# Transposes of the identity in TensorE's prologue waits, q/k products of step 0 moved ahead of it, and another order of the first expert scalings

## The chip, the cores and the metric

One core of one Trainium2 chip. The metric is the device time of one execution in microseconds. "TensorE" is PE in the profile, VectorE is DVE, ScalarE is ACT, GpSimd is POOL, SyncE is SP.

## The reference

Input x is (32, 256, 128): 32 batches of 256 tokens with 128 channels. All is in float32.

```python
x = L0_attn_x
xn = _layernorm(x, axis=-1)
x = x + _L0_attn_ref(xn, ...) + _L0_ffn_ref(xn, ...)
# _L0_attn_ref: 16 heads of 8, rotated q and k, decay bias, causal softmax, output projection
# _L0_ffn_ref:
n1 = _layernorm(x, ln1_w, ln1_b)
rw = _gating(n1, smha_sim, smha_gates, 2)              # weights of 8 experts per token
q = einsum('btc,ech,bte->bth', n1, q_proj, rw)         # k and v likewise
attn = softmax(causal(q @ k.T * scale)) @ v
hs = x + einsum('bth,ehc,bte->btc', attn, o_proj, rw)
n2 = _layernorm(hs, ln2_w, ln2_b)
rw2 = _gating(n2, moe_sim, moe_gates, 2)
inter = gelu(einsum('btc,eci->btei', n2, w1))
return hs + einsum('btei,eic,bte->btc', inter, w2, rw2)
```

## The kernel before

Each engine has its own instruction order, written out by hand, and the engines meet at semaphores. An engine works through its order strictly, so an instruction that waits holds all that stands behind it on that engine.

**Prologue.** It loads constants and weights, normalises batches 0 to 2, computes their rotated q and k (`proj` on TensorE, `rotate` on VectorE, in seven links), the gating of batches 0 and 1, and the first pass of scores of batch 0 in six units (`unit1(0, 0, k)`). A row maximum on VectorE follows each unit (`row_max`), and the next unit waits for it. `n1s`, the channels scaled by the gating weights, is made on GpSimd for eight experts; `qk(n, e)` adds expert e's product of q and of k into one PSUM bank (lines 1621 and 1622). `max_T(0)` transposes the maxima (line 1566), `weights_T(b)` the gating weights (line 1523), which ACT then copies out (`evac_weights`, semaphore `rwT_done`) behind the DMAs that it issues itself.

**Attention loop.** 32 steps, one for a batch. Step n on TensorE interleaves the first pass of batch n+1 (`next_max(k)`), the second pass of batch n (`unit2`), the q/k products of batch n (already made for e = 0 to 3 in the prologue where n is 0, by `first_qk`), `pv`, `soft_scores`, the V products `ve`, and the output products `oe`. For each unit of the second pass ACT takes an exponential (line 789) and then writes the seed for the next unit (line 795). The first unit of the first pass also waits until `rotate(n + 2)` has read its bank, and in step 0 nothing of the step starts before `rwT_done` is 2.

**Expert stage.** 16 tiles of 512 tokens in 8 pairs (a, b), 8 experts each. TensorE runs `down(k)` (line 1898) and `up(k + 3)` (line 1884) in turn. ACT takes the gelu of up's result (line 989), VectorE scales it by the gating weights (`scale_gelu`, line 1422), and `down` reads the scaled tile. VectorE also does, between the scalings, the statistics of the norm of a later pair (`layer_norm2`, 17 interruptible pieces, which end at line 1320), the gating of the next pair (31 links, with a call of `beside_gating(k)` behind most of them), and `finish` of the tile before. On ACT the order is fixed by `at`, the number of the gelu in its pair: behind gelus 3 and 4 stand two scalings each of `z2` for tile t (line 841), which wait for the end of the norm; behind gelus 5 and 6 two each for tile t + 1; between gelu 6 and these last two stands the tanh of the gating (line 875), which waits for the subtraction of line 1174.

In pair 0 VectorE's order is: scalings a0, a1, six pieces of the norm, a2, the rest of the norm, the gating with a3 to a7 at links 7, 12, 17, 22 and 27, then b0 and four pieces of the next norm, b1, `finish(a)`, four pieces, b2, and so on.

Of the kernel before, what the change touches and what calls it, by code (L numbers as in the profile page):

```python
# [19 lines left out]
P = 128  # L20
# [38 lines left out]
GATE_LINKS = 21 + 10  # L59
MAX_LINKS = 3  # L60
ATS_CHUNKS = ((0, 1), (1, 1), (2, 2), (4, 2), (6, 2))
GELU_AT = (2, 7, 12, 17, 22, 27)
GATE_MAX_AT = (1, 6, 13, 17)

# [55 lines left out]
def run(steps):  # L120

    for _ in steps:
        pass


def build(nc, x, w_attn, w_o, log_xi, pi_logit, e_logit, ln1_w, ln1_b, ln2_w, ln2_b, sim1, gates1,
# [9 lines left out]
    with ExitStack() as ctx:  # L136
# [7 lines left out]
        ident = sb("ident", [P, P])  # L144
# [100 lines left out]
        ps = ctx.enter_context(nc.psum_tensor("ps", [P, 8, 512], F32))  # L245
# [32 lines left out]
        rwT_done = sem("rwT_done")  # L278
# [738 lines left out]
        def _(dve):  # L1017
# [396 lines left out]
            def scale_gelu(t, e):  # L1414
                k = E * t + e
                dve.wait_ge(gelu_done, k + 1)
                dve.wait_ge((rep2_lo_in, rep2_hi_in)[e // (E // 2)][t % 2], 16 * (t // 2 + 1))
                if k >= 2:
                    dve.wait_ge(moe_out, k - 1)
                else:  # L1420
                    dve.wait_ge(oe_out, NB)
                dve.tensor_tensor(hgs[:, k % 2], hg[:, k % 4], rep2[t % 2][e // (E // 2)][:, e % (E // 2)], ALU.mult  # L1422
                                  ).then_inc(hgs_done, 1)
# [10 lines left out]
            def pair(g):  # L1434
                a, b = 2 * g, 2 * g + 1
                scale_gelu(a, 0)
                scale_gelu(a, 1)
                if g:
                    finish(a - 1)
                else:  # L1440
                    norm = layer_norm2(2)
                    for _ in range(6):
                        next(norm, None)
                    scale_gelu(a, 2)
                    run(norm)

                def beside_gating(k):
                    if k in GELU_AT[(g == 0):]:
                        scale_gelu(a, 2 + GELU_AT.index(k))

                if g + 1 < NP:
                    gating(g + 1, BP, 1, gate2, LG2(g + 1), LG2(g + 1)[:, :, E], 2, beside_gating)
                else:
                    for k in GELU_AT:
                        beside_gating(k)
                norm = layer_norm2(g + 3) if g + 3 < NP else iter(())
                for e in range(E):
                    scale_gelu(b, e)
                    if e == 1:
                        finish(a)  # L1460
                    for _ in range(4):
                        next(norm, None)
                run(norm)
# [6 lines left out]
        @block.tensor  # L1470
        def _(pe):
            mm = pe.matmul

            def plant_seeds():
                pe.wait_ge(cast_done, CASTS)
# [93 lines left out]
            def unit2(n, u, k):  # L1569

                Q, i = divmod(k, 3)
                if k == 0:
                    pe.wait_ge(max_in, 16 * NF * (n + 1))
                if not isinstance(n, int) or UNITS * n + k >= 1:
                    pe.wait_ge(seed_done, UNITS * n + k)
                for h in range(2 if i < 2 else HG):
                    hh = HG * Q + (2 * i if i < 2 else 0) + h
                    for f in range(NF):
                        bank = ps[:, S2[f]]
                        if i < 2:  # L1580
                            ins = mm(bank[:, h * S:(h + 1) * S], kst[ROWS[f], u, hh, 0:P], qst[ROWS[f], u, hh, :],  # L1581
                                     start=False, stop=True, skip_group_check=True)
                        else:
                            ins = mm(bank[:, h * P:(h + 1) * P], kst[ROWS[f], u, hh, P:S], qst[ROWS[f], u, hh, P:S],
                                     start=False, stop=True, skip_group_check=True)
                ins.then_inc(s2_out, 1)
# [27 lines left out]
            def qk(n, e):  # L1614

                pe.wait_ge(n1s_done, E * n + e + 1)
                if e == 0:

                    pe.wait_ge(ve_done, n)
                    pe.wait_ge(v_done, min(n + 2, NB) if isinstance(n, int) else n + 2)  # L1620
                mm(ps[:, QKB, 0:S], wq[:, e], n1s[:, e], start=(e == 0), stop=(e == E - 1), skip_group_check=True)  # L1621
                ins = mm(ps[:, QKB, S:2 * S], wk[:, e], n1s[:, e], start=False, stop=(e == E - 1),  # L1622
                         skip_group_check=True)
                if e == E - 1:
                    ins.then_inc(qk_out, 1)
# [105 lines left out]
            def step(n, u, n_x):  # L1731
                f, g = n + 2, n + 3

                def next_max(k):
                    if n_x:
                        unit1(n + 1, 1 - u, k, f if n_x >= 2 else None)

                def first_qk(e):
                    if not isinstance(n, int) or n > 0:
                        qk(n, e)  # L1740

                next_max(0)
                unit2(n, u, 0)
                first_qk(0)
                first_qk(1)
                if n_x == 0:
                    norm_T2(0)
                first_qk(2)
                if n_x >= 2:
                    logits_T(f, u)  # L1750
                if n_x == 0:
                    norm_T2(1)
                next_max(1)
                unit2(n, u, 1)
                if n_x >= 2:
                    logits(f)
                first_qk(3)
                qk(n, 4)
                next_max(2)
                unit2(n, u, 2)  # L1760
                qk(n, 5)
                if n_x == 0:
                    logits2_T(0)
                qk(n, 6)
                next_max(3)
                unit2(n, u, 3)
                qk(n, 7)
                pv(n, u, 0)
                if n_x == 0:
                    logits2(0)  # L1770
                next_max(4)
                unit2(n, u, 4)
                soft_scores(n)
                ve(n, 0)
                out_T(n, 0)
                ve(n, 1)
                ve(n, 2)
                ve(n, 3)
                next_max(5)
                unit2(n, u, 5)  # L1780
                if n_x == 0:
                    norm_T2(2)
                for e in range(4, E):
                    ve(n, e)
                if n_x == 0:
                    norm_T2(3)
                soft_T(n)
                if n_x == 3:

                    norm_T(g, LATER, lambda: pe.wait_ge(s1_read, UNITS * f))  # L1790
                pv(n, u, 1)
                soft_av(n, (lambda: pe.wait_ge(lg_read, f + 1)) if n_x >= 2 else (lambda: None))
                out_T(n, 1)
                if n_x == 0:
                    weights_T2(0)
                if n_x >= 2:
                    proj_v(f, True)
                if n_x >= 2:

                    weights_T(f, lambda: None)  # L1800
                if n_x:
                    max_T(n + 1)
                att_T(n)
                if n_x == 3:
                    proj(g, LATER, lambda: None)
                if n_x >= 2:

                    pe.wait_ge(rwT_done, f + 1)
                if n_x:
                    pe.wait_ge(mT_done, n + 2)  # L1810
                oe(n, 0)
                oe(n, 1)
                att_out(n)
                oe(n, 2)
                oe(n, 3)
                if n_x == 0:
                    logits2_T(1)
                for e in range(4, E):
                    oe(n, e)
                if n_x == 0:  # L1820
                    logits2(1)
# [10 lines left out]
            logits(0)  # L1832
            proj_v(0, False)
            plant_seeds()
            norm_T(1, FIRST, lambda: pe.wait_ge(lg_read, 1))
            proj(1, FIRST, lambda: pe.wait_ge(rot_chain, 2))
            weights_T(0, lambda: None)
            pe.wait_ge(rows_in, 16 * N_ROWS)
# [4 lines left out]
            logits(1)  # L1843
            proj_v(1, False)
            unit1(0, 0, 2)
            unit1(0, 0, 3)
            unit1(0, 0, 4)
            pe.wait_ge(ld_w, 16 * N_W)
            qk(0, 0)
            qk(0, 1)  # L1850
            unit1(0, 0, 5)
            qk(0, 2)
            qk(0, 3)
            max_T(0)
            norm_T(2, LATER, lambda: pe.wait_ge(s1_read, UNITS))
            proj(2, LATER, lambda: None)
            weights_T(1, lambda: pe.wait_ge(rwT_done, 1))
            pe.wait_ge(rwT_done, 2)
            step(0, 0, 3)
            step(1, 1, 3)  # L1860
            with pe.Fori(1, NB // 2 - 2) as j:
# [106 lines left out]
```

## Time and profile before

| what | us |
|---|---|
| median of 3 runs | 1212.77 (1212.22 to 1213.09) |
| the profiled execution's own time | 1212.19 |
| its span, first to last instruction | 1210.40 |
| mean granted clock of TensorE | 0.994 of full |
| TensorE busy / VectorE / ACT / POOL | 1161.8 / 1018.8 / 717.7 / 245.9 |
| prologue | 0 to 60.13 |
| step 0 | 60.13 to 89.33 |
| step 1 | 89.33 to 117.50 |
| expert stage | from 963.61 |

The span is what the profile shows; the execution's own time is longer by the start and end around it. Stages are told by TensorE's instructions: step n + 1 begins with the first mask product of its first pass. In a row, the number behind a name is how many instructions it merges, and the time in brackets is how long the engine was idle before and who ended it.

### The profile page before, as it was taken

Reading aid. Unit: us, or ns where it says so; the run is one execution under the profiler, and the core shown is the slowest. Engines: PE = TensorE matmul, PEld = TensorE weight load, DVE = VectorE, ACT = ScalarE, POOL = GpSimd, SP = SyncE. Lnnn points to the kernel's source line nnn. Section 1 sums busy time; section 2 is a strip of 40 time slices with the busy share of each in tenths; the row PEclk is TensorE's granted clock in tenths of the full one; section 3 lists DMA queues with packets and bytes.
Section 4 is the critical chain, followed back from the end, with each engine's and each line's share of the span. In section 5 each row is a group of like instructions: output and inputs, shape, how many; then the busy total and the mean of one; then the engine's idle time right before and its main releaser. Section 6 shows DMA issues by size and latency. Waiting matters only on the chain.

```text
span 1210.4 us, 33207 instructions
## 1 busy us (share of the span) xinstructions
PE 1161.8 (96%) x10652; PEld 896.3 (74%) x10652; DVE 1018.8 (84%) x3687; ACT 717.7 (59%) x1292; POOL 245.9 (20%) x374
## 2 busy tenths in 40 slices
PE   2599999999999999999999999999999999999998
PEld 1377777778777788777777777777877667777776
DVE  8889999999999999999999998999876577777664
ACT  5166666666666656666666666666557745555532
POOL 5222222222222232222222222223322000000000
PEclk9989999999999999999999999999999999999999
DMA  4443233333323333233333323333331234444453
GB/s 109 129 125 91 90 94 106 104 108 89 94 93 91 90 94 91 94 92 89 94 106 107 103 90 93 92 91 91 95 93 54 96 151 165 174 176 168 172 189 120
DMA packets 103113, 133.01 MB, mean 110 GB/s; under 512 B 13576, under 2 KB 82424, under 8 KB 94864
## 3 DMA queue, kind: packets, MB, share of 16 engines
q1 hardware_dynamic: 100548, 130.72, 34.6%
q10 hardware_dynamic: 2508, 1.58, 0.5%
q8 instruction: 31, 0.51, 0.2%
q14 instruction: 26, 0.21, 0.1%
HBM read 109.12 MB, written 21.54 MB: 108 GB/s over the span
## 4 chain that ended last, share of the span: by engine, by line
PE 77%; DVE 14%; issue 6%; ACT 1%; ACTq 1%; DVEq 1%; DMA 1%; POOL 0%; SPq 0%; POOLq 0%
PE ps L1621 10%; PE ps L1667 10%; PE ps L1898 9%; PE ps L1622 9%; PE ps L1884 9%; PE ps L1631 5%; PE ps L1494 3%; PE ps L1598 3%; PE ps L1581 2%; PE ps L1557 2%; PE ps L1547 2%; PE ps L1544 2%; DVE att L1249 1%; PE ps L1554 1%; PE ps L1603 1%
## 5 line engine op out<-in xcount | busy, mean ns | idle before, releaser
L1223 DVE TENSOR_REDUCE mx<-ps 128x4 f32<-128x1024 f32 (+1 forms) x192 | 234.8, 1223 | 35.8 <-PE ps L1557 20.7
L789 ACT ACTIVATE pr<-ps 128x1024 f32<-128x1024 f32 x192 | 196.7, 1024 | 77.1 <-PE ps L1581 54.3
L637 POOL TENSOR_TENSOR n1s<-rep,n1T 128x256 f32<-128x256 f32 x256 | 177.3, 731 | 297.8 <-DVE mpart L1237 280.7
L795 ACT ACTIVATE ps<-trn 128x1024 f32<-128x1024 bf16 x191 | 196.5, 1029 | 5.1
L1898 PEld LDWEIGHTS ps<-w2s,ats 128*128 128x128 f32 x1024 | 131.4, 191 | 53.4 <-issue 43.9
L1621 PE MATMUL ps<-n1s,wqk 128*128 128x256 f32 x512 | 164.7, 404 | 1.3 <-issue 1.3
L1622 PE MATMUL ps<-n1s,wqk 128*128 128x256 f32 x512 | 153.8, 382 | 0.0
L989 ACT ACTIVATE n1s<-ps 128x512 f32<-128x512 f32 x128 | 76.6, 598 | 121.3 <-PE ps L1884 120.2
L1898 PE MATMUL ps<-w2s,ats 128*128 128x128 f32 x1024 | 136.1, 276 | 2.9 <-DVE ats L1422 2.8
L1631 PE MATMUL ps<-wv,n1s 128*128 128x128 f32 x1024 | 133.1, 278 | 0.0
L1884 PE MATMUL ps<-rep,w1s 128*128 128x512 f32 x256 | 130.7, 594 | 0.0
L1631 PEld LDWEIGHTS ps<-wv,n1s 128*128 128x128 f32 x1024 | 124.3, 192 | 4.9
L1667 PE MATMUL ps<-wop,ats 128*128 128x128 f32 x1024 | 126.6, 277 | 0.0
L1667 PEld LDWEIGHTS ps<-wop,ats 128*128 128x128 f32 x1024 | 119.6, 192 | 5.7 <-DVE ats L1274 4.6
L1622 PEld LDWEIGHTS ps<-n1s,wqk 128*128 128x128 f32 x512 | 98.4, 192 | 13.8
L1621 PEld LDWEIGHTS ps<-n1s,wqk 128*128 128x128 f32 x512 | 89.3, 195 | 26.0 <-issue 15.9
L742 ACT ACTIVATE n1T<-xzT,lnp 128x256 f32<-128x256 f32 x32 | 19.2, 600 | 108.2 <-POOL n1s L637 108.2
L1274 DVE TENSOR_TENSOR ats<-rep,ps 128x512 f32<-128x512 f32 (+1 forms) x160 | 81.1, 573 | 0.0
L1598 PE MATMUL ps<-pr,vst 128*32 128x256 f32 x1024 | 68.5, 385 | 0.6 <-ACT pr L789 0.6
L644 POOL TENSOR_TENSOR zt<-xn,rstd 128x256 f32<-128x256 f32 x32 | 20.6, 643 | 215.8 <-DVE rstd L1048 215.8
L656 POOL TENSOR_TENSOR bs<-hs,xa 128x256 f32<-128x256 f32 x32 | 23.3, 728 | 200.2 <-DVE hs L1290 200.2
L1422 DVE TENSOR_TENSOR ats<-n1s,stk 128x512 f32<-128x512 f32 x64 | 44.0, 688 | 14.0 <-PE ps L1898 13.9
(229 smaller groups left out, 2051.4 us busy)
## 6 DMA issues: line engine op xcount, KB each, us to landing
rep<-scr_rw SPq DMA_DIRECT2D x32, 1024.0 KB, 5.6
stk<-scr_rw SPq DMA_DIRECT2D x16, 1024.0 KB, 8.2
scr_parts<-parts SPq DMA_DIRECT2D x64, 192.0 KB, 5.8
stk<-scr_parts SPq DMA_DIRECT2D x248, 48.0 KB
rots<-scr_rw SPq DMA_DIRECT2D x8, 1024.0 KB, 4.8
wqk<-scr_rw SPq DMA_DIRECT2D x8, 1024.0 KB, 8.7
stk<-scr_parts SPq DMA_DIRECT2D x248, 32.0 KB
xt<-in_x SPq DMA_DIRECT2D x32, 128.0 KB, 2.1
```

Of the source, the lines that this page charges most:

```text
L637: pool.tensor_tensor(n1s[:, e], rep[:, par, e], n1T[:, par], ALU.mult).then_inc(n1s_done, 1)
L789: act.activation(pr[:, Q, :, i], ps[:, S2[0]:S2[0] + NF], ACT.Exp).then_inc(exp_done, 1)
L795: act.activation(ps[:, S2[0]:S2[0] + NF], seeds[:, kind:kind + 1].broadcast_to((P, NF, 512)), ACT.Copy).then_inc(seed_done, 1)
L1223: dve.tensor_reduce(mx[:, min(i, 1)].rearrange("p (f h) -> p f h", f=NF)[:, :, h:h + n], ps[:, S1[0]:S1[0] + NF].rearrange("p f (h t) -> p ...
L1274: dve.tensor_tensor(ats[:, e:e + ne], rep[:, u, e:e + ne], ps[:, G0:G0 + 1, 0:S].broadcast_to((P, ne, S)), ALU.mult).then_inc(ats_done, 1)
L1598: mm(ps[32 * h:32 * h + 32, PVB, 0:S], vst[:, u, 0, HH * f + HG * Q + h], pr[:, Q, f, h // 2, (h % 2) * S:(h % 2 + 1) * S], start=(f == 0) ...
L1621: mm(ps[:, QKB, 0:S], wq[:, e], n1s[:, e], start=(e == 0), stop=(e == E - 1), skip_group_check=True)
L1622: ins = mm(ps[:, QKB, S:2 * S], wk[:, e], n1s[:, e], start=False, stop=(e == E - 1), skip_group_check=True)
L1631: ins = mm(ps[:, QKB, i * D:(i + 1) * D], n1s[:, e, i * P:(i + 1) * P], wv[:, e], start=(e == 0 and i == 0), stop=(e == E - 1), skip_group ...
L1667: ins = mm(ps[:, G1, i * D:(i + 1) * D], ats[:, e, i * P:(i + 1) * P], wop[:, e], start=(e == 0 and i == 0), stop=(e == E - 1), skip_group ...
L1884: mm(ps[:, UP[k % 4]], w1s[:, e], n2T[t % 8], start=True, stop=True).then_inc(up_out, 1)
L1898: ins = mm(ps[:, MOE[t % 2], i * D:(i + 1) * D], hgs[:, k % 2, i * P:(i + 1) * P], w2s[:, e], start=(e == 0 and i == 0), stop=(e == E - 1) ...
```

## The change

TensorE transposes the identity matrix 64 times into a part of a PSUM bank that nothing reads: 24 behind the seeds, 8 ahead of `proj(1)`, 16 behind unit 2 of the first pass, 8 behind unit 3 and 8 behind unit 4. The products of q and k of batch 0 for experts 4 to 7 move from step 0 to the prologue (4 and 5 ahead of the transpose of the maxima, 6 and 7 around `proj(2)`). The wait for `rwT_done` 2 moves behind the first unit of both passes of step 0. In pair 0 of the expert stage VectorE scales a3 after five more pieces of the norm, a4 after all of it, and a5, a6, a7, b0 and b1 inside the gating at links 4, 9, 14, 19 and 24.

```diff
--- before.py
+++ after.py
@@ -59,6 +59,7 @@
 GATE_LINKS = 21 + 10
 MAX_LINKS = 3
 ATS_CHUNKS = ((0, 1), (1, 1), (2, 2), (4, 2), (6, 2))
+GELU_FIRST = (4, 9, 14, 19, 24)
 GELU_AT = (2, 7, 12, 17, 22, 27)
 GATE_MAX_AT = (1, 6, 13, 17)
 
@@ -1439,13 +1440,17 @@
                     finish(a - 1)
                 else:
                     norm = layer_norm2(2)
-                    for _ in range(6):
-                        next(norm, None)
-                    scale_gelu(a, 2)
-                    run(norm)
+                    for k, more in enumerate((6, 5, 13)):
+                        for _ in range(more):
+                            next(norm, None)
+                        scale_gelu(a, 2 + k)
+
+                early = ((a, 5), (a, 6), (a, 7), (b, 0), (b, 1))
 
                 def beside_gating(k):
-                    if k in GELU_AT[(g == 0):]:
+                    if g == 0 and k in GELU_FIRST:
+                        scale_gelu(*early[GELU_FIRST.index(k)])
+                    elif g and k in GELU_AT:
                         scale_gelu(a, 2 + GELU_AT.index(k))
 
                 if g + 1 < NP:
@@ -1455,7 +1460,8 @@
                         beside_gating(k)
                 norm = layer_norm2(g + 3) if g + 3 < NP else iter(())
                 for e in range(E):
-                    scale_gelu(b, e)
+                    if g or e >= 2:
+                        scale_gelu(b, e)
                     if e == 1:
                         finish(a)
                     for _ in range(4):
@@ -1470,6 +1476,11 @@
         @block.tensor
         def _(pe):
             mm = pe.matmul
+
+            def turn_ident(times):
+
+                for _ in range(times):
+                    pe.transpose(ps[:, G1, 3 * P:4 * P], ident[:], ident[:])
 
             def plant_seeds():
                 pe.wait_ge(cast_done, CASTS)
@@ -1741,6 +1752,8 @@
 
                 next_max(0)
                 unit2(n, u, 0)
+                if isinstance(n, int) and n == 0:
+                    pe.wait_ge(rwT_done, 2)
                 first_qk(0)
                 first_qk(1)
                 if n_x == 0:
@@ -1755,16 +1768,16 @@
                 if n_x >= 2:
                     logits(f)
                 first_qk(3)
-                qk(n, 4)
+                first_qk(4)
                 next_max(2)
                 unit2(n, u, 2)
-                qk(n, 5)
+                first_qk(5)
                 if n_x == 0:
                     logits2_T(0)
-                qk(n, 6)
+                first_qk(6)
                 next_max(3)
                 unit2(n, u, 3)
-                qk(n, 7)
+                first_qk(7)
                 pv(n, u, 0)
                 if n_x == 0:
                     logits2(0)
@@ -1832,7 +1845,9 @@
             logits(0)
             proj_v(0, False)
             plant_seeds()
+            turn_ident(24)
             norm_T(1, FIRST, lambda: pe.wait_ge(lg_read, 1))
+            turn_ident(8)
             proj(1, FIRST, lambda: pe.wait_ge(rot_chain, 2))
             weights_T(0, lambda: None)
             pe.wait_ge(rows_in, 16 * N_ROWS)
@@ -1843,19 +1858,25 @@
             logits(1)
             proj_v(1, False)
             unit1(0, 0, 2)
+            turn_ident(16)
             unit1(0, 0, 3)
+            turn_ident(8)
             unit1(0, 0, 4)
+            turn_ident(8)
             pe.wait_ge(ld_w, 16 * N_W)
             qk(0, 0)
             qk(0, 1)
             unit1(0, 0, 5)
             qk(0, 2)
             qk(0, 3)
+            qk(0, 4)
+            qk(0, 5)
             max_T(0)
             norm_T(2, LATER, lambda: pe.wait_ge(s1_read, UNITS))
+            qk(0, 6)
             proj(2, LATER, lambda: None)
+            qk(0, 7)
             weights_T(1, lambda: pe.wait_ge(rwT_done, 1))
-            pe.wait_ge(rwT_done, 2)
             step(0, 0, 3)
             step(1, 1, 3)
             with pe.Fori(1, NB // 2 - 2) as j:
```

## Rows read from the trace of the kernel before

**Rows 1.** The page: engines' shares of the chain that ended last.

```profile
PE 77%; DVE 14%; issue 6%; ACT 1%; ACTq 1%; DVEq 1%; DMA 1%; POOL 0%; SPq 0%; POOLq 0%
```

**Rows 2.** Stretches: length, engines' busy time (instructions), granted clock, DMA share, GB/s.

```profile
45.27:48.85 3.58, 3.58 (x8) 2.47 (x8) 3.48 (x10) 0.00 (x0) 3.58 (x6) 1.00 0.15 46
55.42:57.50 2.08, 2.01 (x4) 1.11 (x4) 1.77 (x13) 0.00 (x0) 0.00 (x0) 0.52 0.05 12
60.13:69.20 9.07, 8.30 (x55) 4.75 (x56) 8.76 (x26) 6.25 (x9) 0.00 (x0) 0.50 0.89 278
89.33:117.50 28.17, 28.08 (x283) 22.36 (x283) 25.92 (x94) 17.98 (x33) 7.24 (x11) 1.00 0.31 86
971.80:974.00 2.20, 0.04 (x1) 0.04 (x1) 1.96 (x10) 1.98 (x5) 0.00 (x0) 1.00 0.77 275
```

**Rows 3.** Timeline of TensorE, prologue: start, length, instructions, [idle before <- releaser].

```profile
27.05 0.66 PE L1486 MATMUL ps<-ident,xn 128*128 128x128 f32 x2 [6.13 <-POOL zt L644]
27.51 0.63 PE L1486 MATMUL ps<-ident,zt 128*128 128x128 f32 x2
...
30.05 2.07 PE L1494 MATMUL ps<-xzT,wa 128*128 128x256 f32 x4 [1.91 <-ACT xzT L735]
...
40.78 0.61 PE L1544 MATMUL ps<-mask_r,mask_l 64*128 64x512 bf16 x2 [2.65 <-DVE mx L1223]
...
45.27 1.19 PE L1621 MATMUL ps<-n1s,wqk 128*128 128x256 f32 x2 [1.31 <-issue]
...
50.25 0.59 PE L1621 MATMUL ps<-n1s,wqk 128*128 128x256 f32 x2
...
53.39 0.29 PE L1566 MATMUL ps<-identb,mpart 128*128 128x128 bf16 x2 [2.11 <-DVE mpart L1237]
...
55.42 2.01 PE L1494 MATMUL ps<-xzT,wa 128*128 128x256 f32 x4 [1.29 <-ACT xzT L735]
```

**Rows 4.** Step 0: timelines of VectorE and TensorE, pv of step 1, line 1621 alone.

```profile
59.20 0.72 DVE L1139 STREAM_SHUFFLE rots<-ps 128x512 f32<-128x512 f32 x1
...
70.94 1.23 DVE L1223 TENSOR_REDUCE mx<-ps 128x8 f32<-128x1024 f32 x1 [1.47 <-PE ps L1554]
...
77.62 1.23 DVE L1223 TENSOR_REDUCE mx<-ps 128x4 f32<-128x1024 f32 x1 [0.36 <-PE ps L1557]
...
77.08 0.28 PE L1547 MATMUL ps<-mask_r,mask_l 64*128 64x256 bf16 x2
...
100.28 1.07 PE L1598 MATMUL ps<-pr,vst 128*32 128x256 f32 x16
...
60.13:73.00 12.87, 3.58 (x8) 1.85 (x8) 0.65 0.71 221
```

**Rows 5.** VectorE from 965 to 991.2: timeline; its waits (total, times, longest).

```profile
971.82 0.17 DVE L1320 SCALAR_TENSOR_TENSOR nmr<-bmv,rstd 128x8 f32<-128x8 f32 x1
...
982.53 0.28 DVE L1204 TENSOR_TENSOR gt<-gt,gs 128x64 f32<-128x64 f32 x1
...
987.51 0.69 DVE L1422 TENSOR_TENSOR ats<-n1s,stk 128x512 f32<-128x512 f32 x1
...
DVE ats L1422 <- ACT n1s L989: 1.3, 2, 1.1
DVE ats L1422 <- PE ps L1898: 0.2, 1, 0.2
```

**Rows 6.** Timeline of ACT in the first expert pair.

```profile
972.02 0.88 ACT L841 ACTIVATE xt<-hs,nmr,rstd 128x128 f32<-128x128 f32 x2 [3.29 <-DVE nmr L1320]
972.80 0.58 ACT L989 ACTIVATE n1s<-ps 128x512 f32<-128x512 f32 x1
...
976.51 0.25 ACT L875 ACTIVATE gt<-gt 128x64 f32<-128x64 f32 x1
```

**Rows 7.** Timeline of TensorE in the first expert pair.

```profile
973.96 1.16 PE L1898 MATMUL ps<-w2s,ats 128*128 128x128 f32 x8 [2.19 <-DVE ats L1422]
...
988.26 1.16 PE L1898 MATMUL ps<-w2s,ats 128*128 128x128 f32 x8 [0.24 <-DVE ats L1422]
```

## The prediction

> **What bounds the kernel now.** I read the page first: the chain that ended last lies on TensorE for 77 % of the span, on VectorE for 14 % [rows 1]. Then the stretches, to see where the other part is: a step of the attention loop takes 28.17 us, with 28.08 of them busy on TensorE and 25.92 on VectorE [rows 2]. So from step 1 to the last step TensorE sets the pace, and a microsecond won or lost ahead of step 1 stays. The change touches the exceptions: the prologue up to 60.13 us, step 0 (60.13 to 89.33), and the first pair of the expert stage (from 966 us).
>
> In the prologue TensorE mostly waits. The reader is to see what ends each wait (POOL, ACT, DVE), never TensorE itself [rows 3]. In step 0 it is busy without much gap, but at half pace until 69.2: the granted clock is 0.50 there, the lower level, 1.2 GHz [rows 2]. Before 48.85 it was at that pace too, whatever the column says: a pair of q products takes 1.19 us at 45.27 and 0.59 at 50.25 [rows 3].
>
> In the expert stage the waits of TensorE name one big gap, 2.19 us ahead of the down product of expert 3 [rows 7]. The view that matters is another one: VectorE, from 965 to 991 us, waits 1.3 us for ACT (1.1 of it ahead of its first scaling at 965.3) and otherwise only 0.2, and works without a break from there to 991 [rows 5]. So in this stretch VectorE is the bound, and TensorE's gap is its shadow.
>
> **The change, part by part.**
>
> *64 transposes.* Nothing waits for them, but what stands behind them on TensorE does. Two transposes start at 27.05 us and the next two at 27.51, so one costs 0.23 us at 1.2 GHz [rows 3]. A product of 256 columns takes half as long at 2.4 GHz (below), and I take the same for a transpose. At the lower level:
> - 24 of them: 5.5 us, in a wait of 6.13 [rows 3]. Hidden.
> - 8: 1.8 us, in a wait of 1.91. Hidden.
> - 16: 3.7 us, in a wait of 2.65: unit 3 of the first pass would start 0.7 to 1.0 late, and the row maximum that waits for it (VectorE, then the whole chain of gating(1)) as late.
> - 8 and 8: 1.8 us each, ahead of unit 4 and of the first q/k product, in a wait of 1.31 [rows 3] and one like it. The excess of 0.5 falls on q/k products, for which nothing waits yet.
>
> If the transposes raise the clock, all of them take half, all are hidden, and proj(1) (2.07 us at 30.05) takes 1.1. Rotation 1 starts 0.9 sooner, but unit 3 at 40.78 waits for two things at once, the maximum and a load of stacks whose issue follows the weights' transpose. I let it win 0 to 0.6 there and 0.4 from its own half duration: a gain of 0 to 1.1 us. No row shows a stretch of transposes long enough to see the clock react.
>
> The Trainium skill ("TensorE: Matmul & The Clock Gate", section on the PE-mode transpose) says that transposes don't count as TensorE activity the way products do, so the clock would not rise for them: by it the first case holds, a loss of 0.7 to 1.0. No row here decides it.
>
> Between the ends I take the middle, a gain of 0.1 us at the start of step 0.
>
> *The wait for the second weights goes behind the first unit.* It ends the wait at 60.13. But that unit also waits until rotation 2 has read its bank: the shuffle at 59.20 runs to 59.92 [rows 4]. So the start moves from 60.13 to about 60.0, a gain of 0.1.
>
> *Four q/k products leave step 0.* Their q halves alone kept TensorE busy there for 3.58 us [rows 4] and the k halves take no more than that, so TensorE is relieved of some 6 us. What they uncover is VectorE: the row maxima, rotation and gating of step 0 form one chain with waits for TensorE of 1.47 us at 70.94 and 0.36 at 77.62 [rows 4]. The gain can't pass these 1.8 us. It will be less, since TensorE now has little to do between 61 and 69 us (two units every 2.5 us, paced by the maxima) and the clock, low at the start of step 0 in the trace before, has no reason to rise there. At the lower level pv(0), whose first part takes 1.07 us and the whole 1.44 at full clock, takes 2.9 [rows 4]; it begins near 70.0, when the third exponential is ready; unit 4, the soft scores and the first V products follow, and unit 5 starts at 76.0 to 78.0, against 77.08 now [rows 4]. From unit 5 to the end of the step at 89.33 it is 12.25 us either way. So 1.8 better with the clock up, between 1.1 better and 0.9 worse with it down. I take 0.1 better. Prologue and step 0 together: 0.3 us gained (ends: 2.9 gained, 1.6 lost). In the prologue the moved products stand in waits of 2.11 and 1.29 us ahead of 53.39 and 55.42 [rows 3], at 0.9 us each at full clock, and cost nothing.
>
> *The scalings of the first expert pair.* Name them a0 to a7, b0 to b7. The order was a2, rest of the norm, gating with a3 to a7 inside, b0, statistics, b1, finish, two more steps, b2. It becomes a2, five links, a3, rest of the norm, a4, gating with a5, a6, a7, b0, b1 inside, statistics, finish, b2. VectorE's instructions ahead of b2 are the same in number and kind. So b2, at 987.51 now [rows 5], can't come sooner than by the 0.2 us that VectorE waits, and it comes later by each new wait. There are two:
>
> 1. a3 does come sooner, five links of 0.2 us behind a2, near 970.6, and closes the 2.19 us gap of TensorE. But a4 stands directly behind the norm, and a4's gelu stands on ACT behind two scalings of z2 that wait for that same norm. The norm ends at 971.99 [rows 5], plus a3 ahead of it (0.6): 972.6. ACT then needs 0.8 for the two and 0.58 for the gelu [rows 6]: 974.0. VectorE stands idle 1.4 us, where before gating ran.
> 2. a7 follows link 14, right behind the subtraction that the tanh waits for. On ACT the tanh (0.25), two more z2 scalings (0.8) and then a7's gelu (0.6) come in that order [rows 6]. Overlaps taken off that is 1.5 us, less 0.2 that VectorE works: idle 1.3. Before, a7 stood at link 27 and never met it.
>
> Together 2.7, less the wait of 0.2 that it absorbs: b2 slips by 2.6 us (ends: a gain of 0.2, a loss of 2.9), and with it the down product of 988.26 [rows 7]. From there on TensorE is the bound to the end, so nothing gives this back. TensorE also stands almost idle ahead of it. Gating ends 2.7 + 2 x 0.6 later than 982.81 [rows 5], at 986.7; the weights' transpose runs, and the next product waits until 990.8. Before the transpose the product of b1 and one up product are over by 986.4. That is a gap of some 4.4 us with one short transpose in it.
>
> *The clock in that gap.* In the trace a gap of 2.19 us at full clock left it at 1.00 [rows 2, 7], and between 51.3 and 55.4 us, with under a microsecond of work between two waits of 2.11 and 1.29, it fell to the lower level [rows 2, 3]. A gap of 4.4 us with 0.1 of work is on the far side of both, so I expect it to fall. What it costs depends on how long TensorE then works at 1.2 GHz: 3.58 us of unbroken products before 48.85, and 9.1 us with small waits from 60.13 to 69.2 [rows 2]. Half of such a time is lost: 1.8 to 4.5 us. The work behind the gap is unbroken, so I take near the lower end, 2.2.
>
> Sum: 1212.19 (the profiled run; its span 1210.40 and 1.79 around it) - 0.3 + 2.6 + 2.2 = 1216.7. The median of the runs is 0.6 above the profiled run, so on the median 1217.3.
>
> **Rivals.**
> - *A: the expert stage slips but the clock holds.* Same two waits, and the 2.19 us gap, which left the clock up, is the nearer case. +2.6 - 0.3: 1215.1. For it: work on both sides is dense. Against it: the gap is twice as long.
> - *B: the scalings cost nothing.* If ACT reaches the gelus of a4 and a7 in time, b2 stays put, and only prologue and step 0 count: 1212.5, from 1209.9 to 1214.4. Against it: both waits follow from orders that the diff leaves alone on ACT.
> - *C, faster: the clock rises in the prologue and stays up through step 0.* Then the prologue gives up to 1.1 and step 0 1.8, 2.9 in all. It ends faster only where the expert stage slips by less than 0.5: 1209.9. It decides at the start of pv(0): at 2.4 GHz there, or not. For it: the transposes keep TensorE occupied up to 45 us. Against it: the sparse stretch 61 to 69.
> - *D, the change doesn't do what it says: transposes alone don't raise the clock.* Unit 3 comes 0.7 to 1.0 late and the first q/k products run at half pace, six of them at 1.7 to 1.8 us up to the transpose of the maxima at 53.39. That makes the prologue 1.0 worse than forecast: 1218.3 with the expert stage as above. For it: four transposes at 27.05 left the products of proj(1) at half pace at 30.05 (2.07 us for four instructions) [rows 3], though four prove little. Against it: they occupy the engine all the same. (The Trainium skill's sentence above speaks for it.)
>
> **How the numbers follow.** The stage that slips with a fallen clock has 0.57 (0.32 as forecast, 1217.3; 0.25 with D, 1218.3), A 0.24, B 0.14, C 0.05. The range runs from 1211.8 to 1219.8: above are 4.5 us of clock cost, below are C and the better half of B. A measurement tells about 0.2 %, 2.4 us, from no change: slower means above 1215.2, faster below 1210.4. Nearly all of the likeliest case and a third of A lie above; the rest of A and most of B within; C and a little of B below. So 0.60 slower, 0.33 the same, 0.07 faster. The likeliest case's own range is 1215.3 to 1219.8.
>
> **What would show it.** After: a3's scaling near 970.6 and no gap ahead of the fourth down product; VectorE waiting for ACT (line of the gelu) twice, 1.4 and 1.3 us; the third down product of the second tile (b2) waiting for VectorE for some 4 us (all less the shift of the stages ahead); a granted clock of 0.50 behind it for 3 to 6 us. In step 0: granted clock 0.50 in part of 60 to 73, step 1 beginning within 1 us of 89.33. In the prologue: f32 products at 0.59 or 1.19 us a pair at 30 us tell whether the transposes moved the clock. The prediction is wrong if VectorE doesn't wait for ACT between 970 and 982.

## The result and the profile after

The changed kernel takes 1216.33 us in the median of 7 runs (1215.58 to 1217.60), against 1212.69 for the kernel before on the same chip: a ratio of 1.0033 with a 95 % interval of 1.0022 to 1.0044. It is slower by 3.6 us. The forecast was 1217.3, slower, from 1211.8 to 1219.8.

The profiled execution took 1216.20 us with a span of 1214.4, 4.0 more than before. Lines in the changed file are higher: 1223 became 1224, 1422 became 1423, 989 became 990, 841 became 842, 1898 became 1919, 1544 became 1555. In the kernels of the experiments they shift by a few more; the names of the tiles stay.

**The expert stage first, since the time went there.** VectorE's timeline in the first pair (start, length, instruction, idle before it and who ended it). These answer to [rows 5]; b2 stood at 987.51.

```profile
970.37 0.69 DVE L1423 TENSOR_TENSOR ats<-n1s,rots 128x512 f32<-128x512 f32 x1
...
973.78 0.69 DVE L1423 TENSOR_TENSOR ats<-n1s,stk 128x512 f32<-128x512 f32 x1 [1.43 <-ACT n1s L990]
...
980.18 0.69 DVE L1423 TENSOR_TENSOR ats<-n1s,stk 128x512 f32<-128x512 f32 x1 [1.31 <-ACT n1s L990]
...
989.90 0.69 DVE L1423 TENSOR_TENSOR ats<-n1s,stk 128x512 f32<-128x512 f32 x1
```

VectorE's waits from 965 to 991.2 us (total, times, longest):

```profile
DVE ats L1423 <- ACT n1s L990: 4.0, 4, 1.4
```

a3 comes at 970.37 without a wait. a4 at 973.78 and a7 at 980.18 each wait for their gelu, 1.43 and 1.31 us. Four waits of 4.0 us replace two of 1.3, and b2 stands 2.39 us later in a kernel whose stages ahead ended 0.16 sooner: a slip of 2.55. ACT's timeline shows what the gelus stood behind, as in [rows 6]:

```profile
972.39 0.88 ACT L842 ACTIVATE xt<-hs,nmr,rstd 128x128 f32<-128x128 f32 x2 [3.81 <-DVE nmr L1321]
973.17 0.57 ACT L990 ACTIVATE n1s<-ps 128x512 f32<-128x512 f32 x1
...
978.64 0.26 ACT L876 ACTIVATE gt<-gt 128x64 f32<-128x64 f32 x1 [2.40 <-DVE gt L1175]
978.81 0.86 ACT L842 ACTIVATE red<-hs,nmr,rstd 128x128 f32<-128x128 f32 x2
979.58 0.57 ACT L990 ACTIVATE n1s<-ps 128x512 f32<-128x512 f32 x1
```

ACT had waited 3.81 us for the norm and 2.40 for the tanh's input, and the gelus of a4 (973.17) and a7 (979.58) stood behind these waits. TensorE's timeline, against [rows 7]:

```profile
971.45 1.05 PE L1919 MATMUL ps<-w2s,ats 128*128 128x128 f32 x8
...
974.57 0.66 PE L1709 MATMUL ps<-ident,xt 128*128 128x128 f32 x4 [1.20 <-ACT xt L842]
...
986.78 0.30 PE L1739 MATMUL ps<-ident,gt 128*64 128x128 f32 x1
990.65 1.87 PE L1919 MATMUL ps<-w2s,ats 128*128 128x128 f32 x8 [3.57 <-DVE ats L1423]
...
995.22 1.16 PE L1919 MATMUL ps<-w2s,ats 128*128 128x128 f32 x8
```

The old gap of 2.19 us is closed: the fourth down product starts at 971.45 in place of 973.96. In its place stand 1.20 us ahead of the transposes at 974.57, and 3.57 ahead of the product of b2. That product then takes 1.87 us in place of 1.16. The next down product stood at 991.22 before and stands 4.0 later. From there to the end both kernels run the same way.

**Then the prologue and step 0.** TensorE's timeline, against [rows 3] and [rows 4]:

```profile
27.11 0.41 PE L1497 MATMUL ps<-ident,xn 128*128 128x128 f32 x2 [1.52 <-POOL zt L645]
...
30.28 1.13 PE L1505 MATMUL ps<-xzT,wa 128*128 128x256 f32 x4 [1.67 <-ACT xzT L736]
...
32.73 0.61 PE L1555 MATMUL ps<-mask_r,mask_l 64*128 64x512 bf16 x2 [0.84 <-DMA stk<-scr_parts]
...
38.42 3.68 PE L1483 MATMUL ps<-ident 128*128 128x128 f32 x16
42.03 0.39 PE L1555 MATMUL ps<-mask_r,mask_l 64*128 64x512 bf16 x2
...
61.21 0.39 PE L1555 MATMUL ps<-mask_r,mask_l 64*128 64x512 bf16 x2 [1.02 <-DVE rots L1140]
...
67.26 0.40 PE L1558 MATMUL ps<-mask_r,mask_l 64*128 64x256 bf16 x2 [2.39 <-DVE mx L1224]
...
71.26 1.76 PE L1609 MATMUL ps<-pr,vst 128*32 128x256 f32 x16
...
76.96 0.28 PE L1558 MATMUL ps<-mask_r,mask_l 64*128 64x256 bf16 x2
...
89.21 0.39 PE L1555 MATMUL ps<-mask_r,mask_l 64*128 64x512 bf16 x2
```

VectorE's row maximum that unit 3 waits for:

```profile
39.77 1.22 DVE L1224 TENSOR_REDUCE mx<-ps 128x4 f32<-128x1024 f32 x1
```

Behind the 24 transposes TensorE is at full clock: the products at 30.28 take 1.13 us instead of 2.07. The 16 transposes at 38.42 run at the lower level again, 0.23 us each, and overhang their wait: the maximum ends at 40.99, and unit 3 starts only at 42.03. Before, it started 0.14 us behind its maximum (39.42 to 40.64). So they hold it by 0.9 us; the other 0.35 of the 1.25 was there before them, since the first unit began at 32.73 in place of 32.37. Step 0 begins 1.1 us later and step 1, at 89.21, 0.12 sooner.

Stretches of the same trace (length, busy time of PE, PEld, DVE, ACT, POOL, granted clock, DMA share, GB/s), against [rows 2]:

```profile
32.73:38.40 5.67, 4.43 (x35) 2.31 (x35) 4.57 (x7) 0.72 (x3) 0.00 (x0) 0.50 0.76 205
...
61.21:66.00 4.79, 2.20 (x33) 1.08 (x33) 4.62 (x8) 4.16 (x7) 0.00 (x0) 0.99 0.66 193
66.00:72.90 6.90, 4.28 (x48) 2.37 (x52) 6.46 (x31) 4.28 (x5) 0.00 (x0) 0.51 0.83 271
...
986.90:990.60 3.70, 0.18 (x1) 0.00 (x0) 3.54 (x20) 0.68 (x2) 0.00 (x0) 1.00 0.16 33
990.65:994.20 3.55, 3.55 (x14) 2.05 (x16) 2.67 (x12) 0.00 (x0) 0.00 (x0) 0.54 0.96 348
```

Three times in these rows the granted clock is low right behind a stretch with little work on TensorE: from 32.73 us, behind waits of 1.67 and 0.84 us with 1.4 us of work between them, in step 0 from 66 us, behind waits of 1.46 and 2.39, and in the expert stage behind the gap of 3.57 us.

### The profile page after: what moved, and what is told of

Its sections match the earlier page's. It is cut to its first block, busy times and chain, and to the rows that moved or that the text cites. A ratio compares the mean times of both kernels' runs of the same rounds, so it can differ in the third digit from the quotient of the medians.

```text
span 1214.4 us, 33336 instructions
## 1 busy us (share of the span) xinstructions
PE 1169.0 (96%) x10716; PEld 905.5 (75%) x10716; DVE 1018.9 (84%) x3687; ACT 716.6 (59%) x1292; POOL 245.4 (20%) x374
## 4 chain that ended last, share of the span: by engine, by line
PE 75%; DVE 15%; issue 6%; ACT 1%; DMA 1%; DVEq 1%; ACTq 0%; POOL 0%; SPq 0%; POOLq 0%
PE ps L1632 10%; PE ps L1678 10%; PE ps L1919 9%; PE ps L1633 9%; PE ps L1905 8%; PE ps L1642 5%; PE ps L1609 3%; PE ps L1505 3%; PE ps L1568 2%; PE ps L1592 2%; PE ps L1558 2%; PE ps L1555 2%; DVE att L1250 1%; PE ps L1565 1%; PE ps L1614 1%
## 5 line engine op out<-in xcount | busy, mean ns | idle before, releaser
L1224 DVE TENSOR_REDUCE mx<-ps 128x4 f32<-128x1024 f32 (+1 forms) x192 | 234.8, 1223 | 36.2 <-PE ps L1568 20.6
```

The source lines that it names most:

```text
L1224: dve.tensor_reduce(mx[:, min(i, 1)].rearrange("p (f h) -> p f h", f=NF)[:, :, h:h + n], ps[:, S1[0]:S1[0] + NF].rearrange("p f (h t) -> p ...
```

## The experiments

All kernels were timed in several rounds with the kernel before on the same chip. The first four ran together (before: 1212.56), then four more (1212.43), then two (1212.44). With spreads of 1 to 2 us in each kernel, half a microsecond between two medians tells nothing.

**1 and 2: which half costs.** `scalings_alone` is the kernel before with the three edits to VectorE's `pair`. `prologue_alone` is the kernel before with all the others.

```diff
 scalings_alone (before, plus)
-                    for _ in range(6):
-                        next(norm, None)
-                    scale_gelu(a, 2)
-                    run(norm)
+                    for k, more in enumerate((6, 5, 13)):
+                        for _ in range(more):
+                            next(norm, None)
+                        scale_gelu(a, 2 + k)
...
+                    if g == 0 and k in GELU_FIRST:
+                        scale_gelu(*early[GELU_FIRST.index(k)])
...
+                    if g or e >= 2:
+                        scale_gelu(b, e)
```

> The kernel before with the new order of the scalings alone. Theory (the two waits for ACT delay b2 and the clock falls in TensorE's gap): +4.4 us on the kernel before (2.55 of slip and 1.85 of half-pace work, as read in the trace after), 1217.0; VectorE waits 1.4 and 1.3 us for ACT between 970 and 982, granted clock 0.5 for some 3.4 us behind the gap. Rival (the loss comes from the prologue's transposes and moved products): within 0.5 us of the kernel before.

Measured: 1216.39 us in six runs, ratio 1.0031 (1.0019 to 1.0043), 3.8 us more than before where 4.4 was expected. The waits of VectorE are the same to the tenth: 4.0 us in four, the longest 1.4. TensorE's gap is 3.57 again, and the granted clock behind it, from 991.3 to 995.0 us, is 0.54.

> The kernel before with the transposes, the moved q/k products and the moved wait, scalings as before. Theory: step 0 begins 1.1 us later and takes 1.2 less, so -0.1 to -0.4 us on the kernel before, 1212.4. Rival: the loss sits here, +3 to +4 us.

Measured: 1212.78, ratio 1.0004 (0.9995 to 1.0013). In its trace step 0 runs from 60.81 to 89.87, so the 1.2 us that step 0 won in the changed kernel's trace aren't there in this one. So the whole loss is that of the scalings, and 64 transposes, four moved products and the moved wait are worth nothing that can be measured.

**3: without the two waits.** `no_wait_for_act` keeps a3 early and moves the others.

```diff
-GELU_FIRST = (4, 9, 14, 19, 24)
+GELU_FIRST = (7, 12, 17, 22, 27)
...
-                    for k, more in enumerate((6, 5, 13)):
+                    for k, more in enumerate((6, 5)):
                         for _ in range(more):
                             next(norm, None)
                         scale_gelu(a, 2 + k)
+                    run(norm)
 
-                early = ((a, 5), (a, 6), (a, 7), (b, 0), (b, 1))
+                early = ((a, 4), (a, 5), (a, 6), (a, 7), (b, 0))
...
-                    if g or e >= 2:
+                    if g or e >= 1:
```

> The changed kernel with a3 still early, but a4, a5, a6, a7, b0 inside the gating at links 7, 12, 17, 22, 27 and b1 behind it, so that neither scaling stands right behind what its gelu waits for on ACT. Work of VectorE ahead of b2 unchanged. Theory (waits, not the early a3, cost the time): b2 near 987.2, no gap over 3 us, clock stays at 1.00, 4.3 us less than the changed kernel: 1212.2. Rival (an early a3 alone speeds up the stage since it closes the 2.19 us gap): 2 us less than that, 1210.2. Rival (the slip comes with any early a3): no change, 1216.3.

Measured: 1212.37, ratio 0.9998 (0.9989 to 1.0007), 4.0 us less than the changed kernel. VectorE's waits for ACT are back at 1.3 us in two. And though the gap of 2.19 us is closed here too, it is no faster than the kernel before. TensorE's waits from 965 to 995 us and its timeline in this run, whose expert stage starts 1.3 us later than before, show where the gap went (line 1710 are the transposes of the norm, 1920 the down products):

```profile
PE ps L1920 <- DVE ats L1423: 1.3, 2, 1.1
PE ps L1710 <- ACT xt L842: 1.2, 1, 1.2
```

```profile
987.00 1.16 PE L1920 MATMUL ps<-w2s,ats 128*128 128x128 f32 x8 [1.10 <-DVE ats L1423]
...
989.37 1.16 PE L1920 MATMUL ps<-w2s,ats 128*128 128x128 f32 x8 [0.24 <-DVE ats L1423]
```

An early a3 gave TensorE its work sooner, and TensorE then waited later on: 1.2 us for ACT's scalings of the norm and 1.10 for VectorE, ahead of the product of b1. Together these are 2.3 us, about the gap of 2.19 again; the 0.24 ahead of b2 was there before. The rival, 2 us from the closed gap, is out.

**4: the slip without the clock.** `fill_the_gap` is the changed kernel with transposes in the gap.

```diff
                         weights_T2(g + 1)
+                        if g == 0:
+                            turn_ident(28)
```

> The changed kernel with 28 more transposes of the identity behind the weights' transpose of the first expert pair, in TensorE's gap of 3.57 us (3.1 us at full clock). Theory (the clock fell because TensorE was idle, and transposes count as work): clock stays at 1.00, b2 as late as before, 1.8 us less than the changed kernel: 1214.5. Rival (transposes don't hold the clock): falls all the same, 1216.3 or later if they run at half pace and overhang the gap.

Measured: 1214.86, ratio 1.0019 (1.0010 to 1.0028), 1.5 us less than the changed kernel, and as much less than `scalings_alone`, which was timed beside it. Its timeline of TensorE:

```profile
987.32 3.22 PE L1483 MATMUL ps<-ident 128*128 128x128 f32 x28
991.05 1.16 PE L1919 MATMUL ps<-w2s,ats 128*128 128x128 f32 x8 [0.52 <-DVE ats L1423]
```

VectorE's four waits are unchanged (4.0 us), b2's product is as late, but it takes 1.16 us, and the granted clock from 985 to 998 us is 1.00. It held in the other runs too, as far as their means tell: 0.991 to 0.993 in all eleven, against 0.986 to 0.991 in the seven of the changed kernel. So the loss splits into about 2.3 us of slip (1214.86 against 1212.56; 2.55 in the traces) and 1.5 of clock, and transposes do hold the clock up.

**5: one wait of the two.** `one_wait_left` takes a4 away from behind the norm and leaves a7 at link 14.

```diff
-GELU_FIRST = (4, 9, 14, 19, 24)
+GELU_FIRST = (7, 10, 12, 14, 19, 24)
...
-                    for k, more in enumerate((6, 5, 13)):
+                    for k, more in enumerate((6, 5)):
...
+                    run(norm)
-                early = ((a, 5), (a, 6), (a, 7), (b, 0), (b, 1))
+                early = ((a, 4), (a, 5), (a, 6), (a, 7), (b, 0), (b, 1))
```

> The changed kernel with a4 at link 7 of the gating and a5, a6 at 10 and 12, so that nothing stands directly behind the norm, while a7 stays at link 14, b0 and b1 at 19 and 24. Theory (the slip is the sum of two waits): the first wait of 1.4 us mostly goes, the second of 1.3 stays; b2 slips 1.1 to 1.7 us against the kernel before, TensorE's gap shrinks to 2.2 to 2.8 us. If the clock holds, 1.1 to 1.7 us on 1212.6: 1214.0. If it falls at such a gap too: 1215.8. Rival (each wait alone would slip everything): 1216.3.

Measured: 1214.60, ratio 1.0018 (1.0009 to 1.0027); without one run at 3039.79 us the median is 1213.82. VectorE's waits, and TensorE's timeline behind the gap:

```profile
DVE ats L1423 <- ACT n1s L990: 2.6, 3, 1.3
```

```profile
989.22 1.16 PE L1920 MATMUL ps<-w2s,ats 128*128 128x128 f32 x8 [3.11 <-DVE ats L1423]
```

2.6 us in three, against 1.3 in two: one wait of 1.3 is left, as the sum of two wanted, and b2 slips by 1.29 us (988.47, in a trace whose expert stage starts 0.33 sooner than before). TensorE's gap is 3.11 us, not 2.2 to 2.8, since TensorE had also run further ahead: its last up product ahead of the gap starts at 984.98 in place of 986.88.

The other eleven runs fall into two heaps: 1211.98, 1212.65, 1212.88, 1213.04, 1213.18, 1213.82, and then 1215.37, 1215.87, 1216.05, 1216.55, 1217.08. The means are 3.3 us apart, and 1214.60 lies between them, so it is no typical time. The profiled run, 1213.18, is of the lower heap, and in it the clock held (1.00 from 988.5 to 993.0). The granted clock over the whole run is 0.991 or 0.992 in each run of the lower heap and 0.987 to 0.989 in each of the upper: the clock was low for longer in the upper one. Where it was low, and whether the gap is what decides, isn't shown, since no run of it was traced; and 3.3 us is twice what the fall costs in experiment 4, so more than one fall may be in it. The slowest four runs of `transposes_alone`, whose expert stage is that of the kernel before, also have low means (0.987 to 0.990, against 0.989 to 0.992 in the other seven).

**6 and 7: the parts of the prologue.** `no_sixteen` is the changed kernel less one line, `transposes_alone` the kernel before with `turn_ident` and its five calls.

```diff
 no_sixteen (changed kernel, less)
             unit1(0, 0, 2)
-            turn_ident(16)
             unit1(0, 0, 3)
```

> The changed kernel without the 16 transposes behind unit 2 of the first pass. Theory (they overhang the wait at half pace and hold unit 3 back by 1.2 us, but step 0 is then shorter by as much since the moved products leave it slack): unit 3 near 41.0, step 0 begins near 60.0 in place of 61.2, step 1 near 88.1 in place of 89.2: 1.1 us less than the changed kernel, 1215.2. Rival (step 0 absorbs it, since VectorE's chain and pv at half pace set its end): 0 to 0.3 less.

Measured: 1216.56 in five runs, ratio 1.0038 (1.0025 to 1.0051): no gain, the rival's case. Unit 3 starts at 41.42 in place of 42.03, step 0 at 60.68 in place of 61.21, and step 1 at 89.43, not sooner than 89.21. The theory lost. Step 1 hardly follows the start of step 0: in the twelve traces step 0 begins between 60.13 and 61.21 and step 1 between 87.96 and 90.46, and the latest starts aren't the latest ends.

> The kernel before with the 64 transposes alone. Theory: unit 3 is held back as in the changed kernel, step 0 begins 1.1 us later and still carries its four products; the clock may be up at its start: +0.5 to +1.5 us, 1213.6. Rival (they warm the clock and pay): -0.5 to -2 us.

Measured: 1212.61, ratio 1.0005 (0.9996 to 1.0014). Step 0 begins at 60.67 and step 1 at 89.35. Not the loss that I expected, nor a gain. In this trace the 16 transposes take 3.31 us, not 3.68, and hold unit 3 by 0.5 us, not 0.9 (it starts at 41.80, behind a maximum that ends at 41.13). And 60.13 was an early start, not the usual one. In `scalings_alone` and `late_norm`, whose prologue is that of the kernel before, step 0 begins with these lines:

```profile
60.93 0.61 PE L1550 MATMUL ps<-mask_r,mask_l 64*128 64x512 bf16 x2 [1.02 <-ACT rwT L771]
```

```profile
60.85 0.61 PE L1551 MATMUL ps<-mask_r,mask_l 64*128 64x512 bf16 x2 [1.02 <-ACT rwT L771]
```

Transfers land at another time in each run. In `late_norm` the first unit waits for its stacks and starts at 33.28, against 32.37 before. In `scalings_alone` it is GpSimd's `n1s`, behind the load of the gating weights, that starts at 45.23 against 44.44. A difference of 0.8 us there is the run's, not the kernel's.

**8: what bounds the pair.** `late_norm` is the kernel before with the order of `no_wait_for_act`, and in pair 0 the next norm's pieces only behind b1, so that some 2.6 us of VectorE's work no longer stand ahead of b2.

```diff
-                    for _ in range(4):
+                    for _ in range(4 if g or e >= 2 else 0):
                         next(norm, None)
```

> The prologue of the kernel before; in the expert stage a3 early, a4 to b0 at links 7 to 27, and in pair 0 the pieces of the norm of pair 3 only from b2 on, so that 2.6 us of VectorE's work no longer stand ahead of b2. Theory (VectorE's work ahead of b2 is what bounds the first pair): b2 2.7 us sooner, TensorE without a gap over 1.2 us, 2 to 3 us less than the kernel before, 1210.0. Rival (TensorE or ACT bound the pair): within 0.5 us of 1212.6.

Measured: 1210.94, ratio 0.9987 (0.9978 to 0.9996), 1.5 us less than the kernel before. That is short of the 2 to 3 us expected, though the interval (0.5 to 2.7) reaches into them. In the traces, measured from the start of the expert stage, b2's scaling comes 2.9 us sooner and the down product of b3 2.1 us sooner. TensorE's only wait from 965 to 995 us is this one:

```profile
PE ps L1705 <- ACT xt L842: 1.2, 1, 1.2
```

The stretch is no longer bound by VectorE, and the 1.2 us are those for the norm's scalings on ACT, which nothing here removed.

**9 and 10: step 0 with the clock held.** `late_norm_new_prologue` is `late_norm` with all the change's edits outside the expert stage. `warm_step_0` adds transposes in the three waits of step 0.

```diff
+                if isinstance(n, int) and n == 0:
+                    turn_ident(12)
                 next_max(1)
...
+                if isinstance(n, int) and n == 0:
+                    turn_ident(20)
                 next_max(2)
...
+                if isinstance(n, int) and n == 0:
+                    turn_ident(11)
                 next_max(3)
```

> The expert stage of late_norm with the prologue and step 0 of the change. Theory (prologue and step 0 of the change are worth nothing: their gain and their loss are below the scatter of the clock's rise): within 0.5 us of late_norm, 1210.9. Rival (they cost or gain a microsecond that the comparison with the kernel before hid): 1209.9 or 1211.9.

Measured: 1210.31, ratio 0.9983 (0.9974 to 0.9992). The two intervals overlap almost wholly, so it stays open whether the new prologue is worth half a microsecond.

> The same with 12, 20 and 11 more transposes of the identity in TensorE's three waits for the maxima in step 0 (1.46, 2.39 and 1.36 us in the trace after). Theory (step 0 falls short of its 1.8 us since the clock falls in these waits and pv runs at half pace): granted clock 1.00 from 61 to 75, unit 5 near 75.5 to 76, step 1 near 88 in place of 89.2, 1.0 to 1.5 us less than late_norm_new_prologue, 1209.6. Rival (VectorE's chain sets the end of step 0 whatever the clock): within 0.3 us of it.

Measured: 1209.28, ratio 0.9977 (0.9968 to 0.9986), 1.0 us less than without them, at the near end of the theory. Step 0 of `late_norm_new_prologue` as a stretch (length, busy time of PE, PEld, DVE, ACT, POOL, granted clock, DMA share, GB/s):

```profile
61.00:75.00 14.00, 9.41 (x107) 5.27 (x108) 13.26 (x45) 10.44 (x15) 0.95 (x2) 0.63 0.65 203
```

and from its timeline of TensorE pv, unit 5 and the start of step 1:

```profile
71.09 1.93 PE L1610 MATMUL ps<-pr,vst 128*32 128x256 f32 x16
...
77.34 0.28 PE L1559 MATMUL ps<-mask_r,mask_l 64*128 64x256 bf16 x2
...
89.59 0.39 PE L1556 MATMUL ps<-mask_r,mask_l 64*128 64x512 bf16 x2
```

The same stretch of `warm_step_0`, and then the same places of its timeline:

```profile
61.00:75.00 14.00, 12.78 (x162) 9.74 (x157) 13.51 (x47) 11.41 (x16) 0.95 (x2) 1.00 0.66 201
```

```profile
70.01 1.07 PE L1610 MATMUL ps<-pr,vst 128*32 128x256 f32 x16
...
75.70 0.28 PE L1559 MATMUL ps<-mask_r,mask_l 64*128 64x256 bf16 x2
...
87.96 0.39 PE L1556 MATMUL ps<-mask_r,mask_l 64*128 64x512 bf16 x2
```

Granted clock 1.00 in place of 0.63, pv in 1.07 us in place of 1.93, and both unit 5 and step 1 1.6 us sooner (0.45 of it from an earlier start of step 0). Step 0 takes 27.37 us (60.59 to 87.96), 1.8 less than the 29.20 of the kernel before, which is the prediction's ceiling, and less than in any other of the traces with four products fewer in it (28.0 to 29.3). The granted clock over the whole run is 0.993 to 0.996 in its eleven runs, 0.990 to 0.993 in those of `late_norm_new_prologue`. This is the fastest kernel of the study, 0.23 % under the kernel before.

## Why the prediction was right

- **VectorE bounds the first expert pair, the gap of TensorE is its shadow.** Right, and shown from both sides: closing the gap alone gave nothing (`no_wait_for_act`, 1212.37), taking VectorE's work away gave 1.5 us (`late_norm`).
- **Two new waits for ACT, 1.4 and 1.3 us, b2 later by 2.6.** Measured 1.43, 1.31 and 2.55. Here the forecast rested on orders written in the kernel and lengths read from the trace, and nothing had to be guessed.
- **The gap of TensorE and the fall of the clock.** 4.4 us with one transpose in it was forecast; it was 3.9, from 986.8 to 990.65 (two small waits of TensorE on the way, 1.20 at 974.57 and 0.43 at 980.91, took some of its lead). The clock fell, as forecast. The cost was mis-sized: 2.2 us was put, and the trace shows 1.6 (4.0 + 0.16 at the product behind, less 2.55), and `fill_the_gap` 1.5. The work behind the gap ran at the lower level for 3.5 us, as short as the shortest row of before, not 4.4.
- **The rest of the difference** from 1217.3 to 1216.33 is the step from the profiled run to the median. I added the 0.6 us of before; the changed kernel's profiled run is only 0.1 under its median. The sum on the profiled run was 1216.7, and it took 1216.20: -0.16 for prologue and step 0 (put at -0.3), 2.55 of slip (2.6) and 1.6 of clock (2.2). The ends of the likeliest case, 1215.3 to 1219.8, are narrower than its parts' ends added up (1214.3 to 1221.8); the text doesn't say how they were drawn in.
- **The start of step 0, 0.2 sooner.** It came 1.1 later in the trace. The 16 transposes ran at the lower level, a case between my two (clock up to 32 us, down from there), and held unit 3 by 0.9, within the 0.7 to 1.0 put for that level. Nor did I see that the first unit can wait for stacks, so the 0.8 us that rotation 1 won went into that wait. But most of the 1.1 need not be the change's: with the prologue of the kernel before, step 0 starts at 60.13, 60.85 and 60.93 in three traces, and 61.21 is only 0.3 behind the later two.
- **Step 0, between 1.1 better and 0.9 worse, unit 5 from 76.0 to 78.0.** Unit 5 came at 76.96. My reason was half wrong: the clock was not low at the start of step 0 (0.99 from 61.21 to 66.00), it fell in the waits for the maxima. The effect on pv had the direction forecast, at 2.2 us for the whole (71.26 to 73.46) in place of 2.9, and `warm_step_0` shows what holding the clock there is worth: 1.0 us. In the trace step 0 took 28.0 us in place of 29.2, 1.2 less where 0.1 was taken, and the start was 1.1 later where 0.2 sooner was taken. That the two gave 0.12 together, near the 0.3 forecast, is luck, and both are of the size by which traces of like kernels differ there (step 0 took 29.06 us in `prologue_alone`).
- **The rivals.** A (the clock holds) had 1215.1, and `fill_the_gap`, which makes it hold, gave 1214.86. B and C are out. D is out: transposes do raise the clock (products at 30.28 in 1.13 us, and in 2.07 or 2.08 in the three traces without the 24) and hold it (`fill_the_gap`, `warm_step_0`). The sentence of the Trainium skill ("TensorE: Matmul & The Clock Gate", section on the PE-mode transpose) that transposes don't count as activity is not borne out here, at least for float32 ones back to back; the measurement decides.

## What to carry to other kernels

When an idle gap of the busiest engine is to be closed, first look whether the engine that it waits for works without a break: then filling the gap early only moves it, and what helps is to take work off the other engine ahead of it. When an instruction is moved forward on an in-order engine, list what its input stands behind on the engine that makes it; if that includes something which waits for the mover's own last result, the two engines take turns idling. And price an idle gap on TensorE with the clock behind it: 28 transposes of a constant, put into a gap that was left in place, won back 1.5 us.

## What the runs showed of the hardware

- Float32 transposes of an identity, 0.12 us each at full clock (28 in 3.22 us), raise TensorE's clock and keep it up: 1.00 behind a gap that otherwise left it at 0.54.
- In the expert stage a gap of 2.19 us left the clock up, and one of 3.57 us was followed by a fall in every trace of a kernel that had it: a granted clock of 0.54 in the changed kernel and in `scalings_alone`, and 0.72 (990.6 to 994.0) in `no_sixteen`. A gap of 3.11 us left it up in the one trace taken, but the runs of that kernel lay in two heaps 3.3 us apart with different mean clocks. So a kernel can differ from itself by more than most edits are worth.
- The length of one gap doesn't tell alone: in the prologue the clock was at 0.50 from 32.73 us though no wait from 28.7 us on was over 1.67. Nor does it fall at this place in every run: with the same transposes ahead, the first mask products of the prologue took 0.61 us in six traces and 0.39 in three (`prologue_alone`, `transposes_alone`, `no_wait_for_act`).
- A fall in the middle of a stage bound by TensorE cost 1.5 us (`fill_the_gap`), and the low clock in step 0 about 1.0 (`warm_step_0`).
